# A fused pre-LN transformer layer on one core: last output-projection group in three steps, second LayerNorm in steps 8 to 11, the gelu pairs four segments apart

## The reference

```python
x = x + attention(layernorm(x), W_qkv, W_out)   # 32 query heads, 16 key/value heads of 64, causal, ALiBi bias
x = x + (gelu((layernorm(x) @ U1) @ V1 + b1) @ U2) @ V2 + b2   # rank 64, hidden width 1024
```

## Time and profile before

| | |
|---|---|
| time, median of 3 runs (lowest to highest) | 3125.69 us (3119.35 to 3127.86) |
| profiled execution: its own time, span | 3124.16 us, 3122.4 us |
| PE busy | 2834.3 us, 91% |
| DVE busy | 2240.8 us, 72% |
| ACT busy | 2167.0 us, 69% |
| POOL busy | 1729.3 us, 55% |
| mean granted clock of TensorE | 0.987 |

### The profile page before, as it was taken

One profiled execution on the slowest core, in us unless ns is written; L12 is line 12 of the kernel. 1 busy time (PEld: TensorE's weight loads), 2 busy tenths in 40 slices (PEclk: granted clock), 3 DMA queues, 4 the chain that ended last, 5 costly groups with the idle time before them and its releaser, 6 DMA issues.

```text
span 3122.4 us, 99572 instructions
## 1 busy us (share of the span) xinstructions
PE 2834.3 (91%) x32328; PEld 1975.6 (63%) x32328; DVE 2240.8 (72%) x7035; ACT 2167.0 (69%) x3828; POOL 1729.3 (55%) x1560
## 2 busy tenths in 40 slices
PE   4899999989989899899999999899898998999986
PEld 1576666766657566666766667666575666666664
DVE  6777677776767777677776777767677776777763
ACT  2676767667677676767767676676776767677683
POOL 1555555555555555555555555555555555555564
PEclk9999999999999999999999999999999999999997
DMA  6232232322223222232322323222232222323210
GB/s 167 64 72 55 56 73 48 79 53 64 62 54 77 48 67 60 56 74 46 78 54 55 74 47 78 54 63 62 54 77 48 67 60 56 74 48 78 55 36 8
DMA packets 220087, 195.25 MB, mean 63 GB/s; under 512 B 41738, under 2 KB 217866, under 8 KB 219274
## 3 DMA queue, kind: packets, MB, share of 16 engines
q1 hardware_dynamic: 219540, 188.32, 25.6%
HBM read 27.73 MB, written 8.39 MB: 12 GB/s over the span
## 4 chain that ended last, share of the span: by engine, by line
PE 30%; issue 28%; POOL 26%; ACT 5%; DVE 5%; POOLq 1%; DVEq 0%; ACTq 0%
POOL p_lo L1063 25%; PE proj L437 13%; PE scores L437 6%; PE o_acc L437 5%; PE max_scores L437 2%; PE ffn_acc L437 2%; ACT h_f L810 1%; ACT L730 1%; DVE max_scores L914 1%; DVE v_lo L837 1%; DVE x_rows L855 1%; ACT p_f L730 1%; ACT L810 1%; PE transposes L559 1%; POOL h_lo L1086 1%
## 5 line engine op out<-in xcount | busy, mean ns | idle before, releaser
L1063 POOL TENSOR_TENSOR p_lo<-p_f,p_hi 128x512 f16<-128x512 f32 x1280 | 1474.1, 1158 | 1103.1 <-ACT p_hi L688 1101.0
L730 ACT ACTIVATE p_f<-scores 128x512 f32<-128x512 f32 x1280 | 756.0, 591 | 432.3 <-PE scores L437 303.7
L688 ACT ACTIVATE p_hi<-p_f 128x512 f16<-128x512 f32 x1280 | 802.3, 627 | 53.4 <-issue 37.1
L914 DVE CUSTOM_DVE_ANT_0 max_scores<-max_scores,causal 128x384 f32<-128x384 f32 (+3 forms) x1184 | 564.2, 508 | 281.9 <-PE max_scores L437 279.5
L437 PE MATMUL scores<-q_hi_lo,k_lo_hi 128*128 128x512 f16 (+3 forms) x2048 | 614.7, 300 | 30.5 <-issue 30.2
L437 PE MATMUL scores<-q_hi_aug,k_hi_aug 128*128 128x512 f16 (+3 forms) x2048 | 587.4, 300 | 0.0
L437 PE MATMUL o_acc<-v_hi_one,p_lo 128*128 128x65 f16 x5120 | 521.3, 195 | 44.7 <-POOL p_lo L1063 44.6
L437 PEld LDWEIGHTS o_acc<-v_hi_one,p_lo 128*128 128x128 f16 x5120 | 473.7, 98 | 81.4 <-issue 42.3
L437 PE MATMUL o_acc<-v_lo,p_hi 128*128 128x64 f16 x5120 | 521.2, 194 | 0.0
L437 PE MATMUL o_acc<-v_hi_one,p_hi 128*128 128x65 f16 x5120 | 521.1, 195 | 0.0
L437 PEld LDWEIGHTS o_acc<-v_lo,p_hi 128*128 128x128 f16 x5120 | 470.5, 99 | 19.7
(11 more groups left out here) (110 smaller groups left out, 5212.0 us busy)
## 6 DMA issues: line engine op xcount, KB each, us to landing
q_hi_aug<-q_pair_hi SPq DMA_DIRECT2D x512, 64.0 KB, 2.0
q_hi_lo<-q_pair_hi SPq DMA_DIRECT2D x512, 64.0 KB, 2.0
q_hi_lo<-q_pair_lo SPq DMA_DIRECT2D x512, 64.0 KB, 2.0
k_hi_aug<-k_pair_hi SPq DMA_DIRECT2D x256, 64.0 KB, 2.0
k_lo_hi<-k_pair_hi SPq DMA_DIRECT2D x256, 64.0 KB, 2.0
k_lo_hi<-k_pair_lo SPq DMA_DIRECT2D x256, 64.0 KB, 2.0
x_rows<-in_L_attn_inputs SPq DMA_DIRECT2D x17, 512.0 KB, 3.8
x_residual<-in_L_attn_inputs SPq DMA_DIRECT2D x16, 512.0 KB, 3.8
```

The source lines that it names most:

```text
L688: return nc.scalar.activation(out_ap, in_ap, ACT.Copy, scale=scale)
L730: nc.scalar.activation(p_f[:, k % 3, :], score_bank[k % 2][:, :], ACT.Exp).then_inc(exp_done, 1)
L914: last = nc.vector.tensor_tensor_reduce(out=bank, in0=bank, in1=causal[:, (T - 1 - qt) * P:S], scale=1.0, scalar=-3e38, op0=ALU.add, op1=A ...
L1063: nc.gpsimd.tensor_tensor(p_lo[:, slot, n, :], p_f[:, k % 3, :], p_hi[:, slot, n, :], ALU.subtract).then_inc(lo_p, 1)
```

## The change

The diff moves work between segments; no operation is added or dropped. Output tiles j = 9, 10 and 11 move from (9, 3), (10, 3), (11, 3) to (9, 1), (9, 4), (10, 2). The second LayerNorm's parts follow them, three segments apart instead of five. The pairs of gelus go from (13, 1), (13, 3), (14, 0), (14, 2) to (12, 0), (12, 4), (13, 3), (14, 2). The products with U2 stand three segments behind their pair, and the last of them in (15, 0). `U2_START` goes from segment number 69 to 63. The order of uses, and with it the alternation of the two proj banks, is worked out again from the tables.

```diff
-RSTD2_AT = {(8 + t, 4): t for t in range(T)}
-LN2_AT = {(9 + t, 1): t for t in range(T)}
-LN2_T_AT = {(9 + t, 2): t for t in range(T)}
-U1_AT = {(9 + t, 4): t for t in range(T)}
-
-FFN_PAIRS = {(13, 1): 0, (13, 3): 1, (14, 0): 2, (14, 2): 3}
-
-U2_PAIRS = {(13, 4): 0, (14, 0): 1, (14, 2): 2, (14, 4): 3}
-U2_START = 13 * SEG + 4
+OUT_AT = {(s, OUT_SEG): s for s in range(KV) if s not in (9, 10, 11)}
+OUT_AT.update({(9, 1): 9, (9, 4): 10, (10, 2): 11})
+
+RSTD2_AT = {(8, 4): 0, (9, 2): 1, (10, 0): 2, (10, 3): 3}
+LN2_AT = {(9, 1): 0, (9, 4): 1, (10, 2): 2, (11, 0): 3}
+LN2_T_AT = {(9, 2): 0, (10, 0): 1, (10, 3): 2, (11, 1): 3}
+U1_AT = {(9, 4): 0, (10, 2): 1, (11, 0): 2, (11, 3): 3}
+
+FFN_PAIRS = {(12, 0): 0, (12, 4): 1, (13, 3): 2, (14, 2): 3}
+
+U2_PAIRS = {(12, 3): 0, (13, 2): 1, (14, 1): 2, (15, 0): 3}
+U2_START = 12 * SEG + 3
...
-                        if n == OUT_SEG and out_in(mode, s):
-                            project_out(s)
+                        if (s, n) in OUT_AT and out_in(mode, OUT_AT[s, n]):
+                            project_out(OUT_AT[s, n])
```

More of the change, by code:

```diff
@@ L129, in projection_order @@
                 uses.append(("k", s))
-            if n == OUT_SEG:
-                uses.append(("out", s))
+            if (s, n) in OUT_AT:
+                uses.append(("out", OUT_AT[s, n]))
             if (s, n) in FFN_PAIRS:
@@ L181, in value, with out_use @@
         return self.i * self.times + self.plus
-def out_use(s):
-    return (s - OUT_LAG) % KV // OUT_GROUP, (s - OUT_LAG) % KV % OUT_GROUP
+def out_use(j):
+    return (j - OUT_LAG) % KV // OUT_GROUP, (j - OUT_LAG) % KV % OUT_GROUP
 def a_slot(s):
@@ L197, in out_before, with out_in @@
     return 16 * i + (kv - OUT_RING) // OUT_GROUP * OUT_GROUP + OUT_GROUP
-def out_in(mode, s):
-    return mode != LAST if s >= OUT_LAG else mode != FIRST
+def out_in(mode, j):
+    return mode != LAST if j >= OUT_LAG else mode != FIRST
 def in_stage(mode, s, lag):
@@ L576, in project_v, with project_out @@
                     last.then_inc(pe_v, 1)
-                def project_out(s):
-                    group, t = out_use(s)
-                    bank = next_proj(("out", s), acc_done, 16 * i + s - OUT_LAG + 1)
+                def project_out(j):
+                    group, t = out_use(j)
+                    bank = next_proj(("out", j), acc_done, 16 * i + j - OUT_LAG + 1)
                     if t == 0:
-                        pe.wait_ge(lo_ot, at(16 * i + s - OUT_LAG + OUT_GROUP))
+                        pe.wait_ge(lo_ot, at(16 * i + j - OUT_LAG + OUT_GROUP))
                     for k in range(OUT_GROUP):
@@ L917, in maxima, with add_out @@
                     last.then_inc(max_done, 1)
-                def add_out(to, s, of):
-                    t = out_use(s)[1]
-                    nc.vector.scalar_tensor_tensor(out=to[:, t, :], in0=proj("out", s)[:, 0:D], scalar=1.0 / WO_SCALE,
+                def add_out(to, j, of):
+                    t = out_use(j)[1]
+                    nc.vector.scalar_tensor_tensor(out=to[:, t, :], in0=proj("out", j)[:, 0:D], scalar=1.0 / WO_SCALE,
                                                    in1=of[:, t, :], op0=ALU.mult, op1=ALU.add).then_inc(acc_done, 1)
@@ L973, in body @@
                             low(qs[1][:, s % 2, :], proj("q", s)[:, :], qs[0][:, s % 2, :], Q_OUT).then_inc(lo_q, 1)
-                        if n == OUT_SEG and out_in(mode, s):
-                            group, t = out_use(s)
-                            dve.wait_ge(pe_op, at(16 * i + s - OUT_LAG + 1))
+                        if (s, n) in OUT_AT and out_in(mode, OUT_AT[s, n]):
+                            j = OUT_AT[s, n]
+                            group, t = out_use(j)
+                            dve.wait_ge(pe_op, at(16 * i + j - OUT_LAG + 1))
                             if group == 0:
@@ L979, in body @@
                                     dve.wait_ge(xres_in, at(16 * (i + 1)))
-                                add_out(xacc, s, xres)
+                                add_out(xacc, j, xres)
                             elif group < KV // OUT_GROUP - 1:
-                                add_out(xacc, s, xacc)
+                                add_out(xacc, j, xacc)
                             else:
@@ L985, in body @@
                                     dve.wait_ge(y_out, at(16 * (i - 1) + FREE))
-                                add_out(x2, s, xacc)
+                                add_out(x2, j, xacc)
                         if mode != FIRST:
-                            if n == OUT_SEG and s in range(OUT_LAG - T, OUT_LAG):
-                                t = out_use(s)[1]
+                            if OUT_AT.get((s, n)) in range(OUT_LAG - T, OUT_LAG):
+                                t = out_use(OUT_AT[s, n])[1]
                                 u = (i - 1) * 4 + t
-                                dve.wait_ge(acc_done, at(16 * i + s - OUT_LAG + 1))
+                                dve.wait_ge(acc_done, at(16 * i + OUT_AT[s, n] - OUT_LAG + 1))
                                 nc.vector.bn_stats(bst2[:, t, :], x2[:, t, :]).then_inc(st2, 1)
```

## The result

The changed kernel takes 3254.26 us (median of 4 runs, 3250.18 to 3261.43), the kernel before 3123.95 beside it: a ratio of 1.042, 95% interval 1.0396 to 1.0445. Slower, as forecast, but 54 us later than the 3200 forecast and past the range's end of 3235. The profiled execution took 3261.43 us around a span of 3259.6, 137 more than that of before; its mean granted clock is 0.966, before it was 0.987.

A forecast was written before the change was run, and what follows sets the result against it. TensorE was taken as the bound, with only its stalls to win or add. New stalls of 14.0 us minus old 8.8 gave +5.2 a pass, x 15 = +78, -2 for the tail: 3200 us, range 3128 to 3235.

The forecast's parts named there:

- the 44.6 and 74.1 us rows: TensorE's waits before the change: attention for p_lo in step 8, 44.6 us; max_scores for previous row maxima, 74.1 us.
- (10, 0) LN2 transpose: Second LN2 transpose shares a bank with the transpose of o and waits for o_t_lo: 1.9 us a pass.
- the old 8.8: Old stalls in steps 10 to 14, all expected to go: 7.41 us idle plus lost issue, 8.8 us a pass.
- the row of o_acc: Attention's waits for p_lo: 44.6 us before, to grow to about 80 through new waits of some 2.2 in (13, 1).
- The tail: Last pass: out tiles ahead of LN2 win 5 us, U2 before the next pair's h products costs 3: -2.
- The chain of (13, 1): Gelu pair of (12, 4) delays p_lo: 6.4 us from table load to p_lo's end, so attention waits 2.4.
- The casts: DVE's second cast of all four pairs priced at 1.37 us, held by POOL's h_lo; at 0.43 the sum falls 1.8.
- slower, but only by the casts at 0.43: Rival: all casts short, +3.4 us a pass, 3177 us; chance 0.25 for 3177 and around.
- Faster: Rival: gelus no longer crowd step 14 and two large waits do not come; about 3090 us, chance 0.10.
- the two large waits: New waits of attention at (13, 1), 2.4 us, and of max_scores at (14, 0), 2.9 us a pass.
- More: Rival: DVE's delays add up in the single maxima bank over seventeen segments; +7 us a pass, 3230 us, chance 0.12.
- No change: Rival: old and new stalls cancel, needing one large wait to vanish and the other to halve; chance 0.08.

The follow-up runs named there:

- e3: Changed kernel with dead matmuls, which nothing reads, ahead of five long TensorE waits in each loop pass: 3194.38 us, ratio 1.0239.
- e1: Kernel before with output tiles and second LayerNorm moved as in the change; gelu pairs, U2 and maxima bank as before: 3129.25 us, ratio 1.0028.
- e7: Changed kernel with DVE waiting for both gelus of a pair before its first cast: 3255.0 us, ratio 1.0418.
- e11: Changed kernel with e8's LayerNorm places, casts and h_lo one segment later, and dead matmuls ahead of two step 8 waits: 3152.05 us, ratio 1.0092.
- e2: Kernel before with only U2_START moved to segment 63, so the row maxima have one bank over seventeen segments: 3147.14 us, ratio 1.0079.
- e4: Kernel before with 9 and 6 dead matmuls ahead of two waits in step 8: 3118.19 us, ratio 0.9991.
- e8: e1 with the second and third LN2 transposes in (10, 1) and (10, 4) and the second U1 product in (10, 3): 3099.47 us, ratio 0.9933.
- e12: e8 with 9 and 6 dead matmuls ahead of two waits in step 8: 3084.2 us, ratio 0.987.
- e6: Changed kernel with DVE's casts and POOL's h_lo one segment behind their gelus: 3205.52 us, ratio 1.0274.
- e9: e8 with DVE's casts and POOL's h_lo one segment behind their gelus: 3140.31 us, ratio 1.0055.

## Why the prediction was right or wrong

**The step that failed** is in the first paragraph: "at a granted clock of 1.00 (the 2.4 GHz level) in every window. So TensorE is the bound and only its stalls can be won or added". The clock could be lost too, by the stalls themselves, and the sum has no term for it. "Every window" is not right by its own rows either: the tail, the last row, has 0.67. e3 fills the stalls and gets 3194 us, the 3200 of the forecast; without the filling it is 3254. The trace of before had the warning: its mean clock is 0.987, its passes differ, 188.3 to 190.7 us but for the last, and in about half of them the clock falls in step 8 (0.90 in the window at 1199.60), right behind the two waits, 2.36 and 1.66 us, of the 44.6 and 74.1 us rows. The pass of the earlier trace rows was a short one. The change added stalls of that size in three more places. The Trainium skill (TensorE: Matmul & The Clock Gate, "A second HAM failure mode: psum-queue depth-cycling") tells of a kernel whose short waits between groups of matmuls, as it cycles through PSUM banks, take the clock back and forth; this trace agrees, 167.2 us at 0.50 in 45 falls, 22 of them behind the waits for the banks of (10, 0) and (14, 0).

**The stalls** came out as forecast, in place and nearly in sum (idle us of the median pass; the forecast ones include 0.17 of issue each):

| place | forecast | measured |
|---|---|---|
| (10, 0) LN2 transpose | 1.9 | 1.89 |
| (10, 2) U1; (11, 0) | 0.7; 0.1 | 1.09; 0 |
| (12, 0) h1; (12, 1) q12; (12, 3) maxima | 0.9; 0.7; 0.85 | 0.68; 0.61; 0.53 |
| (13, 0) k13; (13, 1); (13, 3) | 0.75; 2.4; 0.35 | 0.82; 2.14; 0.09 |
| (14, 0) maxima; (14, 3) | 2.9; 1.0 | 2.67; 0.94 |
| (15, 0) maxima | 1.3 | 0.67 |
| sum | 13.85 | 12.13, with 12 x 0.17 of issue 14.2 |

Less the old 8.8 that makes +5.4 us a pass; e3's passes say 74.5 / 15 = +5.0. With 0.17 added, the largest misses are (10, 2), 1.26 for 0.7, and (15, 0), 0.84 for 1.3; they cancel. At (13, 1) the 2.14 are two waits, 0.77 of max_scores for DVE behind the casts and 1.36 of attention for p_lo. So the row of o_acc grew to 64.9 and not to about 80, and the row of max_scores to 103.8 (forecast: over 100). The transpose waits 15 times (28.3 us; 1.89 each), and no proj waits for k_pair_lo, both as said. The row of o_acc before was not all step 8 either, as the first paragraph has it: 15 waits of 2.36 are 35.4 of its 44.6.

**The tail** is 1.4 us shorter, forecast 2, and that is luck: the terms were -5 for the out tiles ahead of LN2 and +3 for U2 between the pairs. The LayerNorm half alone makes it 10.9 us shorter (e1), and with the gelus it is 9.5 longer again.

**The chain of (13, 1)** was walked rightly. The changed kernel's pair of (12, 4), beside the earlier trace rows:

```profile
1120.73 1.28 ACT L813 ACT_TABLE_LOAD   x1
1122.03 1.27 ACT L813 ACTIVATE h_f<-proj,b_cols 128x512 f32<-128x512 f32 x2
1122.77 0.39 PE L440 MATMUL proj<-xn_t_hi,wqkv_lo 128*128 128x512 f16 x1 [0.82 <-ACT h_f L813]
1123.34 1.15 POOL L1090 TENSOR_TENSOR h_lo<-h_f,h_hi 128x512 f16<-128x512 f32 x1 [4.31 <-DVE h_hi L1015]
1123.41 1.36 DVE L1015 CAST h_hi<-h_f 128x512 f16<-128x512 f32 x1 [0.15 <-ACT h_f L813]
1124.86 1.15 POOL L1090 TENSOR_TENSOR h_lo<-h_f,h_hi 128x512 f16<-128x512 f32 x1 [0.36 <-DVE h_hi L1015]
1125.50 0.39 PE L440 MATMUL max_scores<-k_hi_aug,q_hi_aug 96*128 96x384 f16 x2 [0.77 <-DVE row_max L917]
1125.97 1.15 POOL L1067 TENSOR_TENSOR p_lo<-p_f,p_hi 128x512 f16<-128x512 f32 x1
```

From the load to the end of p_lo are 1125.97 + 1.15 - 1120.73 = 6.39 us (6.4 from the earlier trace rows). The load was to begin 1.45 us into (12, 4); on TensorE that segment starts at 1119.01, so it begins 1.72 in.

**The casts** were right in kind, and wrong in number and weight. Three a pass are long, not four: 49 of 128 over 1 us against 31 before, the mean 779 ns against 676. e7 takes all of them away and leaves the time as it was, but it makes h_lo late as well. So the 1.8 us a pass that the sum and the rival "slower, but only by the casts at 0.43", 3177, put on them is not shown.

**The rivals.** Faster needed the two large waits not to come; they came. "More", 3230, had the size nearer and the reason wrong: the delays did not add up in the maxima's bank. No change needed one large wait to vanish; none did. What e11 adds: four segments apart, the gelus lose even with the clock held, so the sign did not hang on the clock.

**Left open:** which of the waits in a pass takes the clock down in a given pass. In e2, e4 and e8 it fell at the top of the loop, behind the wait of about 2 us there that every version has, in some passes and not in others. In e2 a pass longer by 0.77 us went with a change of the place; by what rule is not shown.

## What to carry to other kernels

Where TensorE is the bound, price a new stall twice: its idle time, and the slow matmuls behind it if the trace shows the clock falling behind a stall of that size anywhere; read the mean clock and all passes, not one good pass. Filling such a stall with matmuls that nothing reads can win time though nothing ends sooner; here it did where half clock was a large sum (e3 and e12, not e4). When work is moved in a queue, look where the instruction behind it becomes late: e6 took two stalls down and got two back one segment on, and e9 took one away and got three others. And part the passes from the start and the tail: e1 looked free because 10.9 us of tail hid 16.8 us of passes.

## What I had not expected of the hardware

Waits of 1.9 to 2.7 us, or two shorter ones close together (0.77 and 1.36 in (13, 1)), in a kernel whose TensorE is 89% busy over the span, take the granted clock to 0.50, for 167.2 us of 2976: behind (10, 0) in 7 of the 15 passes, behind (13, 1) in 11, behind (14, 0) in all, the rest in step 8 and at the top of the loop. The 1.64 and 1.47 us of e6 at (13, 2) and (14, 1) took it down in none. Work added can shorten the time: 570 matmuls more, 60 us less. And with a delay of 0.77 us a pass (e2) the fall of the clock moved from step 8 to the top of the loop, and the passes took 25.9 us more (2863.3 against 2837.4), more than twice the delay (15 x 0.77 = 11.6).
